# A gated mixer: VectorE reads the raw gate from its PSUM bank instead of from a ScalarE copy in SBUF

## What is computed

```python
proj = hidden @ W_in.T                      # gate | x,B,C | dt
gate, hBC, dt = split(proj)
hBC = silu(causal_conv(hBC, conv_w) + conv_b)
xs, B, C = split(hBC)
y = selective_scan(softplus(dt + dt_bias), A_log, xs, B, C) + D * xs
g = y * silu(gate)                          # 2048 channels per token
g = g * rsqrt(mean(g * g) + eps) * norm_w
out = g @ W_out.T
```

## Time and profile before

| | us |
|---|---|
| median of 3 runs | 1448.0 |
| lowest, highest | 1447.71, 1451.81 |
| span of the profiled execution, first to last instruction | 1444.4 |
| mixer stage in it, about | 82 to 478 |

### The profile page before, as it was taken

How to read it: one execution, slowest core, us unless ns; L and a number is a source line. 1 busy time by engine, 2 the same in 40 slices (tenths; PEclk the granted TensorE clock), 3 DMA queues, 4 the chain that set the end, 5 groups by cost and what they waited for, 6 DMA issues and landing times. The chain is left out here.

```text
span 1444.4 us, 16409 instructions
## 1 busy us (share of the span) xinstructions
PE 1208.4 (84%) x4614; PEld 641.6 (44%) x4614; DVE 879.5 (61%) x1244; ACT 593.9 (41%) x1742; POOL 569.6 (39%) x531
## 2 busy tenths in 40 slices
PE   0048899779897699999986898988799787997998
PEld 0014444334453344444434555643485336844443
DVE  7978999389985564246325948729741496504222
ACT  2025454454454232232224546647672476711110
POOL 5562675626665231002002856727651275500000
PEclk9999999999999799999998999989899898997999
DMA  6000000000003400000003000030000000000000
GB/s 253 0 22 1 0 1 1 1 0 0 0 0 120 157 0 1 0 0 0 33 10 136 1 1 0 0 138 1 1 2 1 1 0 0 0 0 8 0 0 29
DMA packets 5481, 33.24 MB, mean 23 GB/s; under 512 B 528, under 2 KB 1936, under 8 KB 3536
## 3 DMA queue, kind: packets, MB, share of 16 engines
q1 hardware_dynamic: 5424, 32.61, 5.8%
HBM read 31.56 MB, written 1.05 MB: 23 GB/s over the span
## 5 line engine op out<-in xcount | busy, mean ns | idle before, releaser
L813 POOL TENSOR_TENSOR decays<-decays,scores 128x768 f32<-128x768 f32 x64 | 124.8, 1953 | 152.0 <-ACT decays L749 152.0
L575 PE MATMUL pg<-h,weights 128*128 (+1 forms) x136 | 66.5, 612 | 85.5 <-PEq L356 82.6
L1998 POOL TENSOR_TENSOR f_pair<-m,weights 128x256 f32<-128x256 f32 x80 | 90.9, 1156 | 92.6 <-DVE m L2019 91.6
L1101 PE MATMUL ph<-h,weights 128*128 x256 | 116.5, 600 | 0.0
L1406 POOL TENSOR_TENSOR prob_latent<-prob_latent,inverse_latent 128x128 f32<-128x128 f32 (+1 forms) x128 | 81.5, 660 | 70.4 <-DVE inverse_latent L1396 70.1
L575 PE MATMUL px<-h,weights 128*128 x136 | 73.3, 664 | 26.1 <-DVE conv L886 26.0
L749 ACT ACTIVATE decays<-pcum,neg_cum 128x256 f32<-128x256 f32 (+1 forms) x256 | 87.7, 449 | 11.4 <-PE pcum L628 11.2
L1246 DVE TENSOR_TENSOR mid<-up,ph 128x512 f32<-128x512 f32 x44 | 30.2, 687 | 98.5 <-ACT up L1158 98.5
L1406 POOL TENSOR_TENSOR prob_gqa<-prob_gqa,inverse_gqa 128x128 f32<-128x128 f32 (+1 forms) x128 | 62.0, 506 | 58.4 <-DVE inverse_gqa L1396 56.8
L1158 ACT ACTIVATE up<-ph 128x512 f32<-128x512 f32 x44 | 26.3, 597 | 140.4 <-PE ph L1101 140.4
L886 DVE SCALAR_TENSOR_TENSOR conv<-px,pp,conv 128x510 f32<-128x510 f32 (+2 forms) x102 | 75.1, 737 | 14.5 <-ACT conv L714 11.6
(11 more groups left out here) (327 smaller groups left out, 3069.6 us busy)
## 6 DMA issues: line engine op xcount, KB each, us to landing
weights<-in_w_mixer SPq DMA_DIRECT2D x2, 2048.0 KB, 18.3
weights<-in_w_moe SPq DMA_DIRECT2D x2, 1536.0 KB, 7.8
moe_rest<-in_w_moe SPq DMA_DIRECT2D x2, 1536.0 KB, 13.9
weights<-in_w_gqa SPq DMA_DIRECT2D x1, 3072.0 KB, 10.2
weights<-in_w_gqa SPq DMA_DIRECT2D x1, 2048.0 KB, 14.7
weights<-in_w_moe SPq DMA_DIRECT2D x1, 1920.0 KB, 9.1
weights<-in_w_mixer SPq DMA_DIRECT2D x1, 1536.0 KB, 11.8
weights<-in_w_moe SPq DMA_DIRECT2D x1, 1152.0 KB, 11.7
```

The lines of the kernel that those rows point to most:

```text
L575: op = nc.tensor.matmul(out[0:m, :], w[:, col + k * m:col + (k + 1) * m], net.h[:, ds(i * PAIR + k * TOK, TOK)], start=(k == 0), stop=(k = ...
L813: nc.gpsimd.tensor_tensor(decays[:, head % 4], decays[:, head % 4], scores[:], ALU.mult).then_inc(decay_scaled, 1)
L1101: op = nc.tensor.matmul(out[:], wt[:, n * D + k * P:n * D + (k + 1) * P], net.h[:, ds(i * PAIR + k * TOK, TOK)], start=(k == 0), stop=(k = ...
L1998: op = nc.gpsimd.tensor_tensor(out[:, :, s, :], src[:, :, 1 - s, :], sin[:, None, s, :].to_broadcast([P, 4, HALF]), ALU.mult)
```

## The change

ScalarE's copy of pg into the gate tile (L737) is removed. VectorE's `silu_gate` reads pg itself as its second input, writes the gate tile, and raises `pg_free`. So the bank is freed by VectorE's product, in place of ScalarE's copy. The semaphore `gate_ready` goes: ScalarE's tanh of tile s now waits for `pg_free` of tile s - 1 (which is also the moment from which `tanh_g` may be overwritten), and `gated` waits for `pg_free` too. The guards of the four gate tiles, which ScalarE held (`g_ready`, `parts_ready`, `pt_ready`), go; the one on `g_ready` moves to VectorE.

```diff
--- before.py
+++ after.py
@@ -532,7 +532,7 @@
         pcum_ready = [sem(f"pcum_ready{n}") for n in range(ST)]
         pcum_free = [sem(f"pcum_free{n}") for n in range(ST)]
         row_cols_ready = sem("row_cols_ready")
-        tanh_g_ready, gate_ready = sem("tanh_g_ready"), sem("gate_ready")
+        tanh_g_ready = sem("tanh_g_ready")
         decay_scaled = sem("decay_scaled")
         y_ready, y_free, g_ready = sem("y_ready"), sem("y_free"), sem("g_ready")
         square_ready, square_used = sem("square_ready"), sem("square_used")
@@ -724,17 +724,9 @@
             def tanh_gate(i, s):
                 act.wait_ge(pg_ready, i * (N + 1) + s + 2)
 
-
-                act.wait_ge(gate_ready, i * N + s)
-                if s >= 4:
-                    act.wait_ge(g_ready, i * N + s - 3)
-                elif s == 0:
-                    act.wait_ge(parts_ready, i + 1)
-                else:
-                    act.wait_ge(pt_ready, i * (N + 2) + 1)
+                act.wait_ge(pg_free, i * (N + 1) + s + 1)
                 nc.scalar.activation(tanh_g[:], pg[:], ACT.Tanh, scale=0.5) \
                     .then_inc(tanh_g_ready, 1)
-                nc.scalar.activation(gate[:, s % 4, :], pg[:], ACT.Copy).then_inc(pg_free, 1)
 
             def exp_decay(i, head):
 
@@ -897,9 +889,10 @@
 
             def silu_gate(i, s):
                 dve.wait_ge(tanh_g_ready, i * N + s + 1)
-                dve.wait_ge(pg_free, i * (N + 1) + s + 2)
-                v.scalar_tensor_tensor(gate[:, s % 4, :], tanh_g[:], 1.0, gate[:, s % 4, :],
-                                       ALU.add, ALU.mult).then_inc(gate_ready, 1)
+                if s >= 4:
+                    dve.wait_ge(g_ready, i * N + s - 3)
+                v.scalar_tensor_tensor(gate[:, s % 4, :], tanh_g[:], 1.0, pg[:], ALU.add,
+                                       ALU.mult).then_inc(pg_free, 1)
 
             def row_cols(i):
                 dve.wait_ge(pt_ready, i * (N + 2) + 1)
@@ -938,7 +931,7 @@
 
                 dve.wait_ge(out_used, i * N + max(s - 1, 0))
                 dve.wait_ge(square_ready, i * N + max(s - 1, 0))
-                dve.wait_ge(gate_ready, i * N + s + 1)
+                dve.wait_ge(pg_free, i * (N + 1) + s + 2)
                 v.tensor_tensor(g[:, s % 2, :], y[:], gate[:, s % 4, :], ALU.mult) \
                     .then_inc(g_ready, 1)
 
```

## The result

| | before | after |
|---|---|---|
| median, us (5 runs each, same chip) | 1448.45 | 1503.84 |
| lowest, highest | 1447.71, 1451.81 | 1493.48, 1504.39 |
| ratio after / before | | 1.037 (95% interval 1.0339 to 1.04) |
| span of the profiled execution | 1444.4 | 1491.5 |
| mixer stage in it (first TensorE instruction to the last sum into x_res) | 82.60 to 476.13, 393.5 | 82.63 to 525.81, 443.2 |

The kernel is 3.7% slower. The direction was forecast, the size was not: +55 us by the medians against +9. The profiled execution of after is the shortest of its five; it is 47.1 us longer than that of before, and the mixer stage alone is 49.7 us longer (443.2 less 393.5); what comes behind the stage is 2.6 us shorter (965.7 against 968.3). What the other four runs of after, 9 to 11 us longer still, did isn't in a trace.

The account below looks back on a forecast made before the run. No single engine bounds the mixer stage; VectorE and TensorE are full in different parts. Per pair +4.9 + 1.0 + 0.0 - 1.3 = +4.6 us, two pairs +9.2: 1448.0 to 1457.2 us, range 1449.5 to 1466.

Parts of the forecast that it names:

- Part 3: Decay product holding g in steps 11 to 13: about +1.0 us per pair, at most 1.5 in eleven steps.
- Part 4: Steps 3 to 9 of a pair: 75.2 us together, a change of 0.0; bounds -2.9 and +3.
- part 6: Edits counted at nothing: semaphore waits, a moved guard, and TensorE's clock, with 9.1 of 10.33 us busy.
- Part 2: Later bank release closes a 10.33 us loop, TensorE standing 1.2 us; steps 10 to 13 lose 4.9 us per pair.
- Part 1: VectorE's gate product reading PSUM takes 0.75 us, 0.78 to the next start; bounds 0.68 and 1.73.
- Part 5: A pair's ends: step 14 -0.4, step 15 gains 0.47, start -0.4; sum -1.3 us per pair, bounds -1.5 and -0.5.
- C: Loop locks onto GpSimd in nearly every step, 6.6 us per pair, or product still held: 1470 us; chance 0.10.
- A: The product's contention ends and TensorE wants the bank late enough: 8.1 us faster, 1440 us; chance 0.07.
- B: A wash: loop costs 4.9 per pair but steps 3 to 9 shrink to 72.3: +0.5 per pair, 1449 us; chance 0.14.
- The signs named beforehand: Profile of the changed kernel: product mean 0.75 us, pg wait some 15 us, steps 10 to 13 10.3 to 10.7 us.

Follow-up runs that it names:

- Experiment 1: The kernel before, its copy kept, with the bank pg freed by VectorE's gate product instead; median 1518.0 us, ratio 1.0464.
- Experiment 6: After and before, each with GpSimd's decay product cut to 32 of 384 columns and sum of squares to 32 of 512; 1445.7 and 1411.4 us.
- before_cut: The kernel before with GpSimd's decay product and sum of squares both cut short; median 1411.4 us, ratio 0.974.
- experiment 2: The kernel before without the copy, bank freed by the tanh's end, the product reading tanh_g twice; median 1453.1 us, ratio 0.9996.
- product_mid: After with VectorE's gate product moved right behind y, ahead of g, xs and x_tok; median 1422.8 us, ratio 0.9868.
- after_no_square: After with GpSimd's sum of squares cut to 32 of 512 columns, the decay product left whole; median 1466.4 us, ratio 1.0154.

## Why the prediction was right in its direction and wrong in its size

The step that failed is the price of GpSimd's holds on the new loop, parts 3 and 4, and of the clock, part 6. They stand in the sum with 1.0, 0.0 and nothing per pair. In the twelve steps of the first pair after is 26 us longer, and 12.9 us of it are holds on the loop and 11.3 the slower clock behind the stalls that they make. Part 4 has the error under it: it compared the new loop with the old steps as measured, which had GpSimd's holds in them.

*Part 2, the later release: right.* The loop was put at 10.33 us and is 10.30 in the steps that nothing holds. TensorE's stall in them is 0.99 against 1.2. (The 0.03 for the semaphore has no row of before under it; in after the weights' load starts 0.05 us behind the product's end, 234.68 to 234.73.) Experiment 1 shows that this part alone makes the kernel slower.

*Part 1, the new form: right in kind, the size a little off.* It is never held, as the means of the two forms in before said. It takes 0.674 us and 0.60 to the next start, not 0.75 and 0.78; these were y's, whose pitch is 0.87 in the new kernel. Both read one tile and one bank, so the bank isn't what makes y longer; y also reads an operand per partition (pp), which may be, and wasn't tested. This gave 0.07 us per step back, nothing beside the rest.

*Part 3, GpSimd against the loop: the mechanism right, the term mis-sized.* I put 1.0 us per pair; the holds on the loop are 12.9. The phase was worked out for L813 and g only. The sum of squares was left out. It follows the decay product on GpSimd without a gap, since it takes the previous step's square, which is ready (in step 10 of after L817 starts at 219.25, when g of this step has only just begun at 219.02). So GpSimd isn't there for 1.8 us but for 3.5, and it reaches from g over xs: in steps 10 and 12 g is held by 0.13 us, less than the 0.3 forecast, and xs by 1.07. Its row was in the trace of before, in the timeline of step 12:

```profile
226.94 1.72 POOL L825 TENSOR_TENSOR square_sum<-square_sum,square 128x512 f32<-128x512 f32 x1
```

It cost nothing there, since the instructions beside it were reciprocals and taps. And the upper bound, 1.5 us in each of eleven steps, 16.5 per pair, was nearer to what came than the 1.0; I took the low end because the phase gave it, and the phase was that of one step.

*Part 4, steps 3 to 9: wrong.* 75.2 us were forecast, 89.8 came (128.34 to 218.15), of which the split above gives 9 to holds and 8 to the clock. The holds also came elsewhere: steps 3 and 6, for which they were forecast, are 11.09 and 10.30 us and not held, and steps 4, 5, 8 and 9, put at 10.35 to 10.5, are 13.70 to 16.35. The bound of +3 was built from one instruction, g, at 0.5 us. Experiment 6 shows the error of thought: I compared the new loop with step lengths that had holds in them (10.74), found that it fits below, and forgot that holds don't go away when the loop gets longer. Without GpSimd's two operations the same seven steps of before take 65.9 us (before_cut, 127.64 to 193.55), and seven free loops, 72.1, are 6.2 more and not 2.9 less.

*Part 5, the ends: right in the sum, in part by luck.* Without step 14 the forecast was -0.9 per pair, -1.8 in all, and -2.2 came: -1.5 and +1.2 at the starts of the two pairs, where -0.4 was put for each, and -0.7 and -1.2 at the tails. Step 14, put at -0.4, gained 0.6 us in the second pair and lost 0.9 in the first, where g and xs are held in it. And something behind the stage does change, against the forecast: it is 2.6 us shorter.

*Part 6, the clock: wrong.* "I count no loss" was worked out for a stall of 1.2 us, and there it holds: in steps 11 and 13, with a stall of 0.99, the clock stays at 1.00. But a held step has a stall of 2.2 us and more (2.18 in step 10, 4.08 in step 5), and behind twelve of the fourteen of those the clock falls to 1.2 GHz for a part of the step, at 1.67 us per step and 2.95 in step 5, 11.3 in the first pair. Parts 3 and 6 were summed as if each had its own price. They go together: what lengthens the stall costs its own length and then, mostly, the clock. 12.9 + 11.3 of the 26.05 us of the first pair are of this kind.

*The rivals.* C, the loop that locks onto GpSimd, was nearest: it had the pattern, with 6.6 us per pair for it about half of the 12.9 and nothing for the clock, and a chance of 0.10 was too little. What spoke against it, "0.3 is what the phase gives", rested on the phase of one step. A failed as forecast: the contention of the product does end, but the later release outweighs it, and in experiment 2 a product held for longer cost the stage no more than 2.9 us. B failed with part 4: steps 3 to 9 grew.

*The signs named beforehand.* The product's mean, yes. The wait of the pg matmuls, 49.0 us for some 15. From y to y in steps 10 to 13 of the first pair, 10.3 in two of them and 13.2 in the other two. g held in steps 11 to 13, no: 0.69 us in 11 and 13, 0.82 in 12. TensorE not full from 205 to 241 us, yes. Steps 3 to 9 near 75 us, no.

## What to carry to other kernels

Where the instruction that frees a PSUM bank stands in its engine's order can decide what an edit is worth: with the gate product behind g and xs, which GpSimd can hold, this one cost 50 us of the stage, and with the product ahead of them it gained some 8. It isn't a rule for every bank: x_tok, which frees pt, moved ahead as well, cost 16.5 us. When an edit lengthens a loop, don't compare the new loop with the old step as measured, but with the old step without its holds, and then add the holds again, at full price and with the clock that the longer stall may cost. Moving one instruction shifts the later ones against the engines that hold them, so an order that looks better by its waits has to be measured; three of the five orders tried here gained nothing or lost.

## What the runs showed of the hardware that I had not expected

Two GpSimd instructions back to back hold two VectorE instructions with two SBUF inputs one after the other, and each lets VectorE go only 0.47 to 0.48 us behind its end (219.29 to 219.76 and 220.96 to 221.44 in step 10). The Trainium skill, page "SBUF — State Buffer", section "SBUF: two separate sides", says that the shared port pair is locked for a whole instruction by whichever starts first. The trace agrees that the engine that comes second is held, in both directions: L805, 1.81 us when alone, takes 2.02 at 206.11 in product_mid, where g has been running since 205.78, and its mean in after is 1906 ns. Who is first isn't always plain from the starts, though: L218 starts 0.21 us behind the first L291 in all 28 cases of the fourteen traces, and in six of them GpSimd is the one that is held (5.15 us), in 22 VectorE (L218 then takes 2.66).

A stall of TensorE can cost more than its length. With 0.99 us in a step of 10.3 the granted clock stayed at 1.00 in all eight such steps of after; with 2.18 us in one of 13.2 the mean was 0.87, and 1.67 us were lost behind it. But the same stall doesn't always do it: 2.19 us in two steps that follow each other left the clock at 1.00 in one (11.50 us) and not in the other (13.19), and 3.14 us in step 10 of after_no_square cost 2.85 us in the first pair (15.31 against 12.46) and nothing in the second. So a single step is no proof of what a stall costs.

The same contention moved the start of the mixer by 13 us between executions (70.05 to 83.3 us) with no edit ahead of it, as much as the smaller effects here. Stage times taken from the trace are free of it; totals are not.
